# One scatter or gather at a time on GpSimd, each behind the landing of the one before

## The chip, the cores and the metric

The kernel runs on one core of a Trainium2 chip. The metric is the device time of one execution in microseconds (us), taken as the median of several runs without the profiler. The core has TensorE (PE, matrix products), VectorE (DVE), ScalarE (ACT), GpSimd (POOL) and SyncE (SP, here only an issuer of DMA transfers). The engines run their own instruction streams in order and meet at semaphores.

## The reference, cut to what matters

One transformer block with adaptive layer norm over x of 32 x 256 x 128 float32 (32 batches of 256 tokens):

```
mod = silu(c) @ wmod                       # six rows of 128 per batch: sa, ca, ga, sb, cb, gb
h = layernorm(x) * (1 + ca) + sa
x = x + ga * attention(h)                  # 16 heads of 8, rms-normed Q and K, gated heads
h = layernorm(x) * (1 + cb) + sb
x = x + gb * experts(h)                    # 32 experts, top 2 of a softmax router

def experts(x):                            # T = 8192 tokens
    rw = softmax(x @ router_w.T)
    vals, idx = top_k(rw, 2)
    w_masked = zeros_like(rw).at[arange(T)[:, None], idx].set(vals)
    for w_e, W_e in zip(w_masked.T, expert_weights):
        acc = acc + (x * w_e[:, None]) @ W_e
```

## The kernel before, in words

**Steps.** The work is a software pipeline over 32 batches. Step s handles batch s in stage 0 (b0), batch s-1 in stage 1 (b1) and so on to b8; there are 40 steps (`STEPS`), of which 0 to 34 are attention steps (`DRAIN` is 35) and 35 to 39 drain steps, and behind them come turns that finish the experts. Every engine has an `attention_step` that lists its tasks in the order in which it runs them. That order is written by hand, engine by engine.

**The experts.** The batches 0 to 29 are sparse: each token's row of h2 (128 floats) is sent to a slot in its expert's region in DRAM (`xs_d`), once per chosen expert. A batch has 2 x 128 tokens and two choices, hence four scatters k = 0 to 3 of 128 rows (64 KB) each, one index per partition from `slot`. Four chunks of batches (0-7, 8-15, 16-23, 24-29) have regions of their own. Behind a chunk a table of units of 128 rows is made, SyncE loads four units at a time (`xs_sb`, L650), TensorE transposes and multiplies them with the expert's weights (L2117, L2132), ScalarE stores them in `ys_d`. Then GpSimd gathers a batch's rows back, again four transfers k = 0 to 3 of 128 rows (`yg`, L921, indices `gidx`), and VectorE weighs and adds them (`combine`, L1620 to L1630). Expert groups run from step 16 on, two in each attention step. In attention steps, gathers of one batch stand in each of steps 25 to 34 (`combined_in(s)`), none earlier. The batches 30 and 31 are computed densely at the end.

**GpSimd's stream.** It does arithmetic on tiles and issues the indirect transfers: `scatter` (L906) and `gather` (L921). In an attention step before the change: gathers k=0 and 1 (of the batch combined in this step); scatter k=3 of b7; `x_plus_bias`(b4, L822), `scale_wo`(b4, L831), `copy_v`(b2, L752), `keep_slot`(b7, L896), `scale_wqkv`(b0, L763); `low_part`(b1, L794); gather k=2; `chosen`(b6, L864), `scale_ln2`(b5, L838), `keep_index`(b6, L881), `chosen_ranks`(b6, L873), `shift_ln2`(b5, L847); `max_lead`, `max_lead_wide`, `max_rest`(b2, L801, L808, L814); gather k=3; scatters k=0 and 1 of b6, `keep_weights`(b8, L888), scatter k=2 of b6, `less_largest`(b6, L855 and L856), and `norm_qk`(b0, L781) twice. A scatter waits for `slot_d` (VectorE's slot numbers, L1500) and adds 16 to `scat[batch's parity]` on landing, 64 per batch; a gather adds 16 to `yg_ld[n % 4]`, 64 per batch. In the steps without gathers only the four scatters remain.

**Who waits for GpSimd.** `norm_qk` gives `qn`, which TensorE transposes early in the next step (`transpose_qk`, L1924); ScalarE (`high_part`, L1070, `middle_part`, L1077), VectorE (`rest_part`, L1386) and GpSimd (`low_part`) split it in three bfloat16 parts, SyncE stores the parts (L602, L605) and loads them as `q_aug` and `k_aug` (L622, L626), and TensorE's `scores_q` (L1937) of the same batch needs them late in that step; VectorE's maxima of these scores (L1397) come ahead of the Newton steps that end in `rstd` (L1313), for which the next `norm_qk` waits. `max_rest` gives `msplit` to TensorE's `transpose_max` (L1946), then ScalarE and a transfer, for `scores_k`. `chosen` gives `mask` to `count_before`; `shift_ln2` gives `h2` to `transpose_h2` (L2020). ScalarE's `router_exp` (L1141) waits for `keep_weights`, and `less_largest` waits for that `router_exp`. TensorE's `probs_v` (L1986) gives four heads at a time to ScalarE's copy `out_transposed` (`oT`, L1095). VectorE copies the units' table (L1545) behind a small matmul of TensorE (L2104).

**SyncE and the queues.** SyncE issues the loads and stores in a written order; it waits for the scatters only ahead of a chunk's first group (`rows_complete`, L639), which stands eight or more steps behind them. `shift_ln2` and `slot_number` also wait for the scatters of the batch two earlier. GpSimd's transfers have a queue of their own, and share the core's 16 DMA engines with SyncE's and ScalarE's.

Of the kernel before, what the change touches and what calls it, by code (L numbers as in the profile page):

```python
# [60 lines left out]
FB = 4  # L61
# [25 lines left out]
def chunk_of(n):  # L87

    return next(k for k in CHUNKS if k.lo <= n < k.hi)
# [131 lines left out]
def build(nc, x, Wq, bq, Wk, bk, Wv, bv, Wo, bo, qn_w, kn_w, router_w, expert_w, c_in, wmod, out):  # L221
# [16 lines left out]
    with ctx:  # L238
# [203 lines left out]
        scat = [sem(f"scat{i}") for i in range(2)]  # L442
# [284 lines left out]
        def _(gp):  # L727
# [165 lines left out]
            def keep_slot(b):  # L893
                wait(gp, slot_d, b.n + 1)
                gp.nop(nofuse=True)
                nc.gpsimd.tensor_copy(slot_all[:, bass.ts(b.n, TOPK * TB)], slot[:, b.par]).then_inc(slota_d, 1)  # L896

            @of_sparse
            def scatter(b, k):

                chunk = chunk_of(b.n)
                if chunk.c >= SETS and b.n == chunk.lo and k == 0:
                    gp.wait_ge(xsT_ps, CHUNKS[chunk.c - SETS].base + CHUNKS[chunk.c - SETS].groups)
                wait(gp, slot_d, b.n + 1)
                gp.nop(nofuse=True)
                nc.gpsimd.indirect_dma_start(xs_d[chunk.set], bass.IndirectOffsetOnAxis(ap=slot[:, b.par, k:k + 1], axis=0),  # L906
                                             h2[:, b.par, k % TB, :], None).then_inc(scat[b.par], 16)

            def gather(n, ks):

                chunk = chunk_of(n)
                if n == chunk.lo and ks[0] == 0:
                    gp.wait_ge(look, 4 * (chunk.c + 1))
                    for i in range(YB):
                        gp.wait_ge(yt_st[i], 16 * groups_until(chunk.base + chunk.groups, i))
                if ks[0] == 0:
                    wait(gp, mix_d, MIX * (n - FB) + 2 * TB)
                gp.nop(nofuse=True)
                for k in ks:
                    pair = n * TOPK * TB + k  # L920
                    nc.gpsimd.indirect_dma_start(  # L921
                        yg[:, n % FB, k, :], None, ys_d[chunk.c],
                        bass.IndirectOffsetOnAxis(ap=gidx[:, pair:pair + 1], axis=0)).then_inc(yg_ld[n % FB], 16)

            def gather_in(s, *ks):

                for n in combined_in(s):
                    gather(n, ks)

            def attention_step(s, ahead, b0, b1, b2, b3, b4, b5, b6, b7, b8):  # L930

                gather_in(s, 0, 1)
                scatter(b7, 3)
                x_plus_bias(b4)
                scale_wo(b4)
                copy_v(b2)
                keep_slot(b7)
                past_first(scale_wqkv, b0)
                low_part(b1)
                gather_in(s, 2)  # L940
                chosen(b6)
                scale_ln2(b5)
                keep_index(b6)
                chosen_ranks(b6)
                shift_ln2(b5)
                max_lead(b2)
                max_lead_wide(b2)
                max_rest(b2)
                gather_in(s, 3)
                scatter(b6, 0)  # L950
                scatter(b6, 1)
                keep_weights(b8)
                scatter(b6, 2)
                less_largest(b6)
                norm_qk(b0, 0)
                norm_qk(b0, 1)

            def drain_step(s, ahead, b0, b1, b2, b3, b4, b5, b6, b7, b8):

                if s == DRAIN:  # L960
                    scatter(b7, 3)
                for k in range(TOPK * TB):
                    scatter(b6, k)
                gather_in(s, 0, 1, 2, 3)
# [1307 lines left out]
```

## Time and profile before

| | us |
|---|---|
| median of 3 runs without the profiler | 832.31 (829.86 to 837.1) |
| span of the profiled execution, first to last instruction | 977.1 |
| TensorE busy in it | 751.6 (77%) |
| VectorE busy | 676.2 (69%) |
| ScalarE busy | 564.5 (58%) |
| GpSimd busy | 507.0 (52%) |
| mean granted TensorE clock, share of full speed | 0.886 |

The profiled execution took longer than those without the profiler. Every duration below is from that one execution. In timeline rows the columns are start, duration, engine, line, operation, output and inputs with shapes, number of instructions merged, and in brackets the idle time of that engine just before and what ended it ("issue" is time in which it waited for nothing that the profile shows, "remote" an event of which the profile doesn't know the sender). Matmul ends are modelled. The duration of a DMA_INDIRECT is GpSimd's time for issuing it, not the movement of the data.

### The profile page before, as it was taken

The numbers are of one execution on the slowest core, as the hardware profiler recorded it, in microseconds if no ns is written. First come the engines' busy times: TensorE is split into PE (matmuls) and PEld (weight loads), VectorE is DVE, ScalarE is ACT, GpSimd is POOL, SyncE is SP. The second block draws the span as 40 slices with busy tenths as digits, with TensorE's granted clock in tenths as the row PEclk, the third lists the DMA queues.
The fourth block names the chain that finished last, engine by engine and source line by source line (L and its number), as shares of the span: only waits on it lengthen the run. The fifth ranks groups of instructions, "written<-read, shape, count | busy, mean of one in ns | idle before, by whom it ended". The sixth has DMA issues, their size and how long they took to land.

```text
span 977.1 us, 23375 instructions
## 1 busy us (share of the span) xinstructions
PE 751.6 (77%) x6334; PEld 512.0 (52%) x6334; DVE 676.2 (69%) x2015; ACT 564.5 (58%) x1300; POOL 507.0 (52%) x846
## 2 busy tenths in 40 slices
PE   4668988988888889998889788887988762524765
PEld 1234655545554566665666555564655551514665
DVE  4757878878786878788888687788876252611556
ACT  3156877776775778877778676676666522512100
POOL 5112455566654555555556666676665535273253
PEclk8579999999997999999999999999898765766888
DMA  2555545466444567767566666665554433754632
GB/s 66 146 146 142 117 115 148 120 150 151 123 115 122 152 168 183 179 175 181 158 179 177 178 161 172 162 167 152 152 154 122 128 108 86 211 154 133 183 81 81
DMA packets 178001, 141.70 MB, mean 145 GB/s; under 512 B 19540, under 2 KB 162612, under 8 KB 177876
## 3 DMA queue, kind: packets, MB, share of 16 engines
q1 hardware_dynamic: 122804, 99.54, 39.8%
q10 hardware_dynamic: 47392, 24.92, 8.8%
q0 software_dynamic: 7680, 15.74, 5.8%
q8 instruction: 57, 0.93, 0.5%
q14 instruction: 68, 0.56, 0.2%
HBM read 81.77 MB, written 57.80 MB: 143 GB/s over the span
## 4 chain that ended last, share of the span: by engine, by line
PE 39%; DVE 15%; issue 14%; DMA 9%; another core or an unknown queue 9%; SPq 7%; ACT 5%; POOL 1%; ACTq 0%; DVEq 0%; POOLq 0%
PE mx_ps L1937 10%; PE st_ps L1972 7%; PE o_ps L1986 6%; DVE negmax L1397 5%; DMA k_aug<-k_d 4%; DMA k_d<-parts 4%; PE st_ps L2132 3%; SPq L650 2%; PE misc L1995 2%; PE misc L1910 2%; SPq L602 2%; ACT pr L1089 2%; PE st_ps L2117 1%; PE misc L2029 1%
## 5 line engine op out<-in xcount | busy, mean ns | idle before, releaser
L1397 DVE TENSOR_REDUCE negmax<-mx_ps 128x2 f32<-128x512 f32 x512 | 339.0, 686 | 123.4 <-PE mx_ps L1937 68.1
L1089 ACT ACTIVATE pr<-st_ps 128x512 f32<-128x512 f32 x512 | 285.2, 599 | 77.9 <-PE st_ps L1972 71.9
L1937 PE MATMUL mx_ps<-k_aug,q_aug 126*128 126x256 bf16 x1024 | 200.1, 287 | 68.0 <-DVE negmax L1397 26.0
L1972 PE MATMUL st_ps<-q_aug,k_aug 128*128 128x256 bf16 x1024 | 190.5, 285 | 0.8 <-ACT ys_sb L1151 0.3
L1986 PE MATMUL o_ps<-pr,v_aug 128*32 128x256 f32 x2048 | 145.7, 404 | 37.4 <-issue 31.4
L921 POOL DMA_INDIRECT yg<-ys_d,gidx x120 | 117.7, 981 | 95.6 <-DVE yb L1627 42.0
L1937 PEld LDWEIGHTS mx_ps<-k_aug,q_aug 126*128 126x128 bf16 x1024 | 84.3, 100 | 158.3 <-issue 148.2
L906 POOL DMA_INDIRECT xs_d<-h,slot x120 | 120.5, 1004 | 59.2 <-DVE slot L1500 33.9
L1972 PEld LDWEIGHTS st_ps<-q_aug,k_aug 128*128 128x128 bf16 x1024 | 101.4, 105 | 30.1 <-issue 11.1
L1986 PEld LDWEIGHTS o_ps<-pr,v_aug 128*32 128x32 f32 x2048 | 57.3, 112 | 89.2 <-issue 69.5
L1095 ACT ACTIVATE oT<-o_ps 128x256 f32<-128x256 f32 x128 | 49.2, 384 | 77.7 <-remote 43.3
L781 POOL TENSOR_TENSOR qn<-qkvg,rstd 128x256 f32<-128x256 f32 x64 | 39.1, 635 | 83.3 <-DVE rstd L1313 83.3
L2117 PE MATMUL st_ps<-ident,xs_sb 128*128 128x128 f32 x248 | 41.9, 299 | 34.8 <-DMA xs_sb<-xs_d 22.0
L794 POOL TENSOR_TENSOR parts<-rest,parts 128x512 bf16<-128x512 f32 x32 | 37.1, 1158 | 52.5 <-ACT parts L1077 52.5
L1910 PE MATMUL misc<-wq_b,hT 128*128 128x400 f32 x128 | 58.5, 545 | 1.0 <-ACT hT L1028 0.9
L1151 ACT ACTIVATE ys_sb<-mx_ps 128x512 f32<-128x512 f32 x25 | 14.9, 596 | 65.7 <-remote 42.6
L2117 PEld LDWEIGHTS st_ps<-ident,xs_sb 128*128 128x128 f32 x248 | 32.2, 156 | 37.8 <-issue 37.1
L1995 PE MATMUL misc<-ident,oT 128*128 128x128 f32 x256 | 43.3, 297 | 10.9 <-ACT oT L1095 7.4
L1146 ACT ACTIVATE xsT<-st_ps 128x512 f32<-128x512 f32 x62 | 36.5, 596 | 24.2 <-PE st_ps L2117 20.1
L2132 PE MATMUL mx_ps<-we,xsT 128*128 x200 | 37.2, 347 | 13.8 <-ACT xsT L1146 9.9
L2132 PE MATMUL st_ps<-we,xsT 128*128 x296 | 42.6, 288 | 2.8 <-issue 1.4
L1366 DVE TENSOR_TENSOR qkvg<-misc,bias_p 128x400 f32<-128x400 f32 x64 | 36.0, 564 | 12.0 <-PE misc L1910 6.7
(192 smaller groups left out, 1280.3 us busy)
## 6 DMA issues: line engine op xcount, KB each, us to landing
xs_sb<-xs_d SPq DMA_DIRECT2D x248, 64.0 KB
ys_d<-ys_sb ACTq DMA_DIRECT2D x62, 256.0 KB
q_aug<-q_d SPq DMA_DIRECT2D x64, 192.0 KB
mod_o<-mod_d SPq DMA_DIRECT2D x32, 256.0 KB
bias_p<-bias_d SPq DMA_DIRECT2D x32, 200.0 KB
q_d<-parts SPq DMA_DIRECT2D x32, 192.0 KB, 2.1
k_d<-parts SPq DMA_DIRECT2D x32, 192.0 KB, 2.5
k_aug<-k_d SPq DMA_DIRECT2D x64, 96.0 KB
```

What stands on the lines that cost most here:

```text
L906: nc.gpsimd.indirect_dma_start(xs_d[chunk.set], bass.IndirectOffsetOnAxis(ap=slot[:, b.par, k:k + 1], axis=0), h2[:, b.par, k % TB, :], No ...
L921: nc.gpsimd.indirect_dma_start(yg[:, n % FB, k, :], None, ys_d[chunk.c], bass.IndirectOffsetOnAxis(ap=gidx[:, pair:pair + 1], axis=0)).the ...
L1089: nc.scalar.activation(pr[:, h % PR], st_ps[score_bank(b, h)][:], ACT.Exp, scale=SCALE).then_inc(exp_d, 1)
L1095: nc.scalar.activation(oT[:, g, :], o_ps[:, 0:NT], ACT.Copy).then_inc(oT_d, 1)
L1397: v.tensor_reduce(negmax[:, :, h], mx_ps[h % 2][:], AX.X, ALU.max, negate=True).then_inc(mx_d, 1)
L1910: t_.matmul(bank[:, 0:QKVG], hT[:, t * P:(t + 1) * P], wq_b[:, b.par], start=True, stop=True).then_inc(qkv_ps, 1)
L1937: last = t_.matmul(mx_ps[h % 2][:, qc], q_aug[b.par][0:MROW, h, qc * P:(qc + 1) * P], k_aug[b.par][0:MROW, h, :], start=True, stop=True)
L1972: last = t_.matmul(st_ps[score_bank(b, h)][:, kc], k_aug[b.par][:, h, kc * P:(kc + 1) * P], q_aug[b.par][:, h, :], start=True, stop=True)
L1986: last = t_.matmul(o_ps[32 * j:32 * j + VW, 0:NT], v_aug[b.par][:, kc, h, :], pr[:, h % PR, kc, :], start=(kc == 0), stop=(kc == TB - 1))
L1995: last = t_.transpose(bank[:, g * P:(g + 1) * P], oT[:, g, qc * P:(qc + 1) * P], ident[:])
L2117: last = t_.transpose(in_bank(g)[:, k * P:(k + 1) * P], xs_sb[:, g % XB, k, :], ident[:])
L2132: last = t_.matmul(out_bank(g)[:, k * P:(k + 1) * P], xsT[g % XB][:, k * P:(k + 1) * P], we[:, bass.ds(columns[k], P)], start=True, stop=True)
```

## The change

In the attention steps each scatter and each gather waits, before it is issued, until the scatter or gather issued last by GpSimd has landed (`behind_last`). They stand in other places of GpSimd's list: never two of them without a wait, and arithmetic between most. Scatter k=2 of a batch moves into the following step, beside k=3. The drain steps and the turns behind them issue as before, without that wait; the first drain step issues scatter k=2 as well.

```diff
+            asked = []
+
+            def behind_last():
+
+                if asked:
+                    gp.wait_ge(*asked[-1])
+
             @of_sparse
-            def scatter(b, k):
-
+            def scatter(b, k, alone=False):
+
+                if alone:
+                    behind_last()
...
+                asked.append((scat[b.par], 64 * b.nth + 16 * (k + 1)))
+
+            def gather(n, ks, alone=False):
+
+                if alone:
+                    behind_last()
...
+                    asked.append((yg_ld[n % FB], 64 * (n // FB) + 16 * (k + 1)))
+
+            def gather_in(s, *ks, alone=False):
 
                 for n in combined_in(s):
-                    gather(n, ks)
+                    gather(n, ks, alone)
 
             def attention_step(s, ahead, b0, b1, b2, b3, b4, b5, b6, b7, b8):
 
-                gather_in(s, 0, 1)
-                scatter(b7, 3)
+                scatter(b7, 2, True)
                 x_plus_bias(b4)
                 scale_wo(b4)
                 copy_v(b2)
                 keep_slot(b7)
                 past_first(scale_wqkv, b0)
+                gather_in(s, 0, alone=True)
                 low_part(b1)
-                gather_in(s, 2)
+                scatter(b7, 3, True)
                 chosen(b6)
                 scale_ln2(b5)
                 keep_index(b6)
+                gather_in(s, 1, alone=True)
                 chosen_ranks(b6)
                 shift_ln2(b5)
+                gather_in(s, 2, alone=True)
                 max_lead(b2)
                 max_lead_wide(b2)
                 max_rest(b2)
-                gather_in(s, 3)
-                scatter(b6, 0)
-                scatter(b6, 1)
+                gather_in(s, 3, alone=True)
+                scatter(b6, 0, True)
                 keep_weights(b8)
-                scatter(b6, 2)
                 less_largest(b6)
+                scatter(b6, 1, True)
                 norm_qk(b0, 0)
                 norm_qk(b0, 1)
 
             def drain_step(s, ahead, b0, b1, b2, b3, b4, b5, b6, b7, b8):
 
                 if s == DRAIN:
+                    scatter(b7, 2)
                     scatter(b7, 3)
```

## Rows read from the trace of the kernel before

**Rows 1.** The page: the chain that ended last, shares by engine.
```profile
PE 39%; DVE 15%; issue 14%; DMA 9%; another core or an unknown queue 9%; SPq 7%; ACT 5%; POOL 1%; ACTq 0%; DVEq 0%; POOLq 0%
```

**Rows 2.** Windows by stage: steps 7-13, 14-24, 25-34, the rest; length, busy per engine.
```profile
core 0: us, PE busy (x) PEld busy (x) DVE busy (x) ACT busy (x) POOL busy (x), PEclk, DMA share, GB/s
137.50:285.30 147.80, 129.71 (x1153) 80.48 (x1153) 118.84 (x363) 105.92 (x253) 86.46 (x160) 0.93 0.52 131
285.30:534.20 248.90, 220.81 (x2022) 150.47 (x2022) 201.50 (x601) 186.38 (x432) 136.42 (x254) 0.96 0.63 164
534.20:785.00 250.80, 203.86 (x1820) 138.08 (x1820) 176.73 (x546) 164.20 (x382) 157.39 (x258) 0.92 0.58 154
785.00:977.10 192.10, 101.71 (x652) 90.33 (x650) 83.96 (x267) 36.74 (x67) 81.64 (x84) 0.74 0.45 131
```

**Rows 3.** Groups of GpSimd by line and form: busy us, mean ns, idle before.
```profile
L906 POOL DMA_INDIRECT xs_d<-h,slot x120 | 120.5, 1004 | 59.2 <-DVE slot L1500 33.9 <-issue 23.1
L921 POOL DMA_INDIRECT yg<-ys_d,gidx x120 | 117.7, 981 | 95.6 <-DVE yb L1627 42.0 <-issue 28.4 <-DMA ys_d<-ys_sb 16.0
...
L855 POOL TENSOR_TENSOR dlg<-lg,top 128x64 f32<-128x64 f32 x29 | 8.5, 295 | 19.1 <-issue 18.7
```

**Rows 4.** Timeline, end of a step without gathers.
```profile
415.87 1.07 PE L1986 MATMUL o_ps<-pr,v_aug 128*32 128x256 f32 x16
415.92 1.02 POOL L906 DMA_INDIRECT xs_d<-h,slot  x1 [1.25 <-DVE slot L1500]
...
418.60 0.98 POOL L906 DMA_INDIRECT xs_d<-h,slot  x1 [0.16 <-issue]
418.78 0.38 ACT L1095 ACTIVATE oT<-o_ps 128x256 f32<-128x256 f32 x1 [1.24 <-remote]
...
419.55 1.44 DVE L1397 TENSOR_REDUCE negmax<-mx_ps 128x2 f32<-128x512 f32 x2 [1.78 <-remote]
```

**Rows 5.** Timeline, head of the step after it.
```profile
421.93 1.22 POOL L781 TENSOR_TENSOR qn<-qkvg,rstd 128x256 f32<-128x256 f32 x2 [1.37 <-DVE rstd L1313]
...
423.30 1.02 POOL L906 DMA_INDIRECT xs_d<-h,slot  x1 [0.15 <-issue]
...
424.04 0.67 DVE L1397 TENSOR_REDUCE negmax<-mx_ps 128x2 f32<-128x512 f32 x1
```

**Rows 6.** Timeline, a step with gathers and the head of the next.
```profile
667.73 1.16 POOL L794 TENSOR_TENSOR parts<-rest,parts 128x512 bf16<-128x512 f32 x1 [1.67 <-ACT parts L1077]
...
678.68 1.01 POOL L921 DMA_INDIRECT yg<-ys_d,gidx  x1 [0.40 <-DVE slot L1500]
...
683.26 0.38 ACT L1095 ACTIVATE oT<-o_ps 128x256 f32<-128x256 f32 x1 [2.62 <-remote]
...
688.33 1.01 POOL L921 DMA_INDIRECT yg<-ys_d,gidx  x1
...
691.95 0.74 POOL L822 TENSOR_TENSOR xga<-x_o,mod_o 128x256 f32<-128x256 f32 x1
```

**Rows 7.** Timeline, drain steps: the first of 16 gathers, and the table's copy.
```profile
800.55 0.98 POOL L921 DMA_INDIRECT yg<-ys_d,gidx  x1 [0.30 <-issue]
...
824.02 0.41 DVE L1545 CAST table<-misc 1x256 int32<-1x256 f32 x1 [21.64 <-remote]
```

**Rows 8.** A lone scatter and the window of its bytes; a gather and its user.
```profile
182.18 1.02 POOL L906 DMA_INDIRECT xs_d<-h,slot  x1
...
183.75:184.00 0.25, 0.25 (x2) 1.00 0.75 262
...
863.65 0.95 POOL L921 DMA_INDIRECT yg<-ys_d,gidx  x1 [0.30 <-issue]
...
866.30 0.48 DVE L1620 TENSOR_SCALAR yw<-yg,p_all 128x128 f32<-128x128 f32 x2 [0.30 <-issue]
```

**Rows 9.** Waits: GpSimd from 130 to 785 us, and one of TensorE's whole span.
```profile
POOL mask L864 <- DVE oh L1459: 49.0, 21, 6.3
...
POOL mlead L801 <- DVE negmax L1397: 25.9, 25, 1.8
...
PEld misc L1946 <- POOL msplit L814: 12.0, 22, 0.8
```

More of the change, by code:

```diff
@@ L907, in scatter @@
                                              h2[:, b.par, k % TB, :], None).then_inc(scat[b.par], 16)
-            def gather(n, ks):
+                asked.append((scat[b.par], 64 * b.nth + 16 * (k + 1)))
+            def gather(n, ks, alone=False):
+                if alone:
+                    behind_last()
                 chunk = chunk_of(n)
@@ L923, in gather @@
                         bass.IndirectOffsetOnAxis(ap=gidx[:, pair:pair + 1], axis=0)).then_inc(yg_ld[n % FB], 16)
-            def gather_in(s, *ks):
+                    asked.append((yg_ld[n % FB], 64 * (n // FB) + 16 * (k + 1)))
+            def gather_in(s, *ks, alone=False):
                 for n in combined_in(s):
-                    gather(n, ks)
+                    gather(n, ks, alone)
             def attention_step(s, ahead, b0, b1, b2, b3, b4, b5, b6, b7, b8):
-                gather_in(s, 0, 1)
-                scatter(b7, 3)
+                scatter(b7, 2, True)
                 x_plus_bias(b4)
```

## The prediction

> **What bounds the kernel now.** I read four views in this order: the chain that ended last, the windows by stage, the waits, and stretches of the timeline. The chain is led by TensorE (39%), but 14% is "issue" and 9% is "another core or an unknown queue" [rows 1]. The windows say how much of the attention steps TensorE does not fill: 147.8 - 129.7, 248.9 - 220.8 and 250.8 - 203.9 us, together 93 us of 647.5, at mean clocks of 0.93, 0.96 and 0.92 [rows 2]. After 785 us it fills only 101.7 of 192.1 us at 0.74.
>
> The timeline shows where these 93 us lie. GpSimd's indirect DMAs take about 1.0 us each (1004 ns for a scatter, 981 ns for a gather) [rows 3]. In a step without gathers three scatters are issued, the first at 415.92, the last at 418.60 us. The matmul group of probs_v ended by its record at 416.94, yet ScalarE's copy of it starts at 418.78 after a wait of 1.24, and VectorE stands 1.78 us until 419.55, both put down to "remote" [rows 4]. So results of TensorE come about 2.4 us later than their records say while scatters follow each other. Behind a lone scatter (423.30) VectorE's next maximum starts at 424.04 with no idle time [rows 5]. In a step with gathers there are two bunches: four transfers from 678.68, with ScalarE waiting 2.62 us until 683.26, and three from 688.33 [rows 6]. Where 16 gathers stand in a row, from 800.55, VectorE waits 21.64 us for a transposition [rows 7]. I count 19 steps without gathers (6 to 24) and 10 with (25 to 34): 19 x 2.4 = 46, 10 x (1.8 + 2.6) = 44, sum 90, which is the 93 us that TensorE doesn't fill.
>
> **The recorded execution is not the timed one.** Its span is 977.1 us, the median is 832.31: 144.8 us less, where what lies around a span would make the time longer. What could vanish without the recorder is the 90 us; the lost clock, (1-0.93) x 147.8 + (1-0.96) x 248.9 + (1-0.92) x 250.8 = 40; in the tail the 21.6 and, by an estimate from the tail's unfilled 90 us, some 35 more. That is 187 us, more than the 145 that must vanish. I therefore take it that the stall behind bunches is mostly the record's, and that the timed execution has at most (187 - 145)/187 = 0.22 of it, unless other losses exist that only the record has. This is the choice on which the forecast hangs.
>
> **The change part by part.** It removes no transfer and adds none: 8 per step with gathers, 4 without. One scatter per step crosses into the next step.
>
> *Steps without gathers.* Removed ahead of norm_qk: scatter k=2, 1.0 + 0.3 us. Added: scatter k=1 waits for the landing of k=0, with keep_weights and less_largest between, three instructions of at most 0.3 us each (295 ns for the longest [rows 3]), about 0.9 with gaps. When does one land? A scatter that starts at 182.18 moves its bytes around 183.75 to 184.0, that is 1.6 to 1.8 us after its start; a gather starting at 863.65 had landed when VectorE used it at 866.30, so by 2.65 [rows 8]. I take 2.2 us from start to semaphore, ends 1.8 and 2.65. The wait is then 2.2 - 1.0 - 0.9 = 0.3 us (0 to 0.8), against 1.3 us of issue moved away. norm_qk waits for VectorE's rstd by 1.37 us in such a step [rows 5], so both vanish. Scatter k=2 takes the place that k=3 had at the head; k=3 now stands behind low_part, ahead of chosen, which waits 49 us over 21 times for one_hot in these stages (2.3 us each) [rows 9]; 1.0 us fits. Sum 0; bounds -0.3 to +0.3 us per step by whether rstd or GpSimd comes last.
>
> *Steps with gathers.* At the head two transfers go: the issue of three took 691.95 - 688.33 = 3.6 us ahead of x_plus_bias [rows 6], now one takes 1.0 + 0.15, while gather k=0 comes back (1.15) behind scale_wqkv. low_part could start 3.6 - 2.3 = 1.3 us earlier. Recorded it waited 1.67 us for ScalarE [rows 6], but with the bunch of that stretch taking no TensorE time, GpSimd itself would be late: low_part heads the road through the parts and the loads to scores_q of the same batch. I count -1.3 us, bounds -1.3 and 0.
> Against this: gather k=3 and scatter k=0 are neighbours, so the landing is waited for openly: 2.2 - 1.0 = 1.2 for 0.3, +0.9 us; scatter k=1 +0.3. Behind it stand keep_weights (router_exp and ScalarE wait for it), less_largest, norm_qk and the whole next head. Between the other neighbours lies 1.0 to 2.5 us of arithmetic after the issue, start to start 2.3 us or more, so at 2.2 they don't wait. Gather k=2 now stands ahead of max_lead, which waits 25.9 us over 25 times, 1.0 each [rows 9]: 1.15 us fits within 0.15 (gather k=1 ahead of chosen_ranks has no one waiting so directly). TensorE waits for max_rest (12.0 us over 22 times [rows 9]), so this 0.15 counts twice over. Sum: -1.3 + 0.9 + 0.3 + 0.3 = +0.2 us per step; with a landing of 1.8: -0.7; with 2.65: each of seven neighbours pays up to 0.4 more, +2.9.
> Total of the forecast case: 10 x 0.2 = 2 us, minus a few us of a remnant of the stall: 0, so 832 us, with 10 x (-0.7) and 10 x 1.2 (2.4 us landing) around it: 822 to 844.
>
> The first drain step gets one scatter more, 1.3 us, on a GpSimd that stands idle for over 10 us there. The rows of 16 and 24 gathers behind the attention steps are not touched.
>
> The Trainium skill (SBUF — State Buffer, "Who interferes with whom") says that only VectorE and GpSimd share a port and that TensorE never waits on anyone. Rows 4 and 7 show TensorE's results late beside GpSimd's transfers, so for the recorded execution the trace contradicts it; by that rule nothing is to be gained from spreading the transfers, which is the forecast case.
>
> **The rivals.**
> A. *The stall behind bunches is real in part.* For it: the record ties it to bunches in every such step, and lone transfers have none. Against it: 187 us must lose 145. Removable are 90 + 40 = 130 us of attention steps. At the share of 0.22 that is 29 us, less 2: 805 us. If the recorder also slows the loads (so that less of the 145 falls to the stall), a share of 0.4 gives 52 us, 782 us. This decides from a share of 0.08 on (10 us).
> B. *The landing waits make GpSimd's own round the longest.* In a step with gathers it is busy 157.4/10 = 15.7 us [rows 2]; with five gaps of 0.3 between neighbouring transfers and an estimate of 0.15 us for each of 13 other hand-overs that is 19.2 us. TensorE's work is 220.8/11 = 20.1 us per step [rows 2]. With landings 2.65 us after the start, eight waits add some 2.9 us: 22.1 us, over TensorE's round by 2.0; with the loads' traffic on the same 16 DMA engines landings may take 3 us, for 24. What waits is TensorE at transpose_max. Price 10 x 2 = 20 us, 852 us; it decides from a landing of about 2.3 us on. Against it: a quiet landing is faster, and the head gets 1.3 us back.
> C. *It does something else than it says:* the awaited value could be reached early, as two batches share a semaphore by parity. The values count 64 per batch and 16 per transfer, in issue order, so each wait is for the last one issued. I leave this at no chance of its own.
>
> **How the numbers follow.** Forecast case 0.41, its own range 822 to 844. A 0.34, centre 805, from 782 to 823. B 0.25, centre 850, from 841 to 870. A measurement of this kernel tells 1% (8 us) from no change. Faster by over 1%: 0.31 of A and 0.04 of the forecast case, 0.35. Slower: 0.22 of B and 0.04 of the forecast case, 0.26. Within: 0.39. The range for 8 in 10 leaves out the lower fifth of A and the upper part of B: 790 to 856.
>
> **What would show it.** In the profile after, "remote" waits of oT and negmax at the ends of steps shrink to under 0.5 us, the clock of the attention steps rises toward 1, and the recorded span falls by 60 to 110 us, far more than the time: this gap shows that the stall is the record's. If time and span fall alike, A holds. Under B, mlead and msplit have no idle time ahead of them in steps 25 to 34, TensorE's wait for msplit there grows beyond 1 us a step, and the idle time ahead of scatter k=0 is over 1.5 us. low_part's wait for ScalarE should grow at the head of gather steps if the 1.3 us is real. The prediction is wrong if the time leaves 822 to 844.

## The result, and the profile after

The changed kernel takes 1000.37 us (992.23 to 1006.21) beside 834.7 us for the kernel before: a ratio of 1.197, 95% interval 1.189 to 1.206. The forecast was 832, within 790 to 856. It was wrong by 168 us, on the side of rival B and far past its price.

One thing is needed to read the numbers below. The kernel before has two speeds, by the chip it runs on. Its recorded trace [rows 1 to 9] has a span of 977.1 us; on two chips of the experiments it took 975 to 979.5 us, on a third 836, and in the measurement of the change 834.7. I call the first kind the 977 chips and the other the 835 chip. The trace of the changed kernel comes from the 835 kind (it has no "remote" wait, and its time came back on that chip), so it must not be held against [rows 2] directly. An experiment below records the kernel before on the 835 chip; its rows take the place of [rows 2] in the comparison.

The groups of GpSimd's transfers in the changed kernel, as in [rows 3] (busy us, mean ns, idle before them and what ended it):

```profile
L915 POOL DMA_INDIRECT xs_d<-h,slot x120 | 121.2, 1010 | 217.5 <-DMA xs_d<-h,slot 112.6
...
L933 POOL DMA_INDIRECT yg<-ys_d,gidx x120 | 119.3, 994 | 93.0 <-DMA yg<-ys_d,gidx 38.1
```

The transfers themselves cost what they did: 1010 and 994 ns against 1004 and 981. The idle time ahead of the scatters rose from 59.2 to 217.5 us. The waits of GpSimd say for what. First the 19 steps without gathers (116.48 to 543.47 us), then seven of the ten with gathers (to 780.21 us); columns: us in total, times, longest:

```profile
POOL xs_d L915 <- DMA xs_d<-h,slot: 76.8, 24, 5.2
POOL dlg L855 <- issue: 31.4, 18, 1.9
...
POOL h L847 <- DMA xs_d<-h,slot: 12.4, 15, 2.7
```

```profile
POOL xs_d L915 <- DMA yg<-ys_d,gidx: 40.7, 14, 5.1
POOL yg L933 <- DMA yg<-ys_d,gidx: 26.0, 14, 3.4
POOL xs_d L915 <- DMA xs_d<-h,slot: 25.2, 13, 4.3
POOL yg L933 <- DMA xs_d<-h,slot: 10.0, 6, 1.9
```

In the seven steps the four landing waits sum to 101.9 us, 14.6 a step. The last row of the first list is a wait that the kernel before had too (`shift_ln2`, for the scatters of the batch two earlier). It sums to 12.4 us here, to 9.9 with one landing wait a step (below) and to 0.5 in the new order without any, so it comes with the waits; scatter k=3 stands shortly ahead of shift_ln2.

GpSimd's timeline shows one such step, its transfers alone:

```profile
644.62 1.02 POOL L915 DMA_INDIRECT xs_d<-h,slot  x1 [4.21 <-DMA xs_d<-h,slot]
645.67 1.22 POOL L781 TENSOR_TENSOR qn<-qkvg,rstd 128x256 f32<-128x256 f32 x2
647.70 1.00 POOL L915 DMA_INDIRECT xs_d<-h,slot  x1 [0.81 <-DMA xs_d<-h,slot]
...
651.31 1.02 POOL L933 DMA_INDIRECT yg<-ys_d,gidx  x1 [0.16 <-issue]
...
655.16 0.99 POOL L915 DMA_INDIRECT xs_d<-h,slot  x1 [1.46 <-DMA yg<-ys_d,gidx]
...
659.67 1.64 POOL L933 DMA_INDIRECT yg<-ys_d,gidx  x1 [1.95 <-DMA xs_d<-h,slot]
...
663.99 1.09 POOL L933 DMA_INDIRECT yg<-ys_d,gidx  x1 [1.52 <-DMA yg<-ys_d,gidx]
...
667.43 0.97 POOL L933 DMA_INDIRECT yg<-ys_d,gidx  x1 [1.31 <-DMA yg<-ys_d,gidx]
...
672.76 1.00 POOL L915 DMA_INDIRECT xs_d<-h,slot  x1 [4.36 <-DMA yg<-ys_d,gidx]
...
677.79 1.02 POOL L915 DMA_INDIRECT xs_d<-h,slot  x1 [2.75 <-DMA xs_d<-h,slot]
```

Read it by the starts: 647.70 - 644.62 = 3.08 us, then 3.61, 3.85, 4.51, 4.32, 3.44, 5.33 and 5.03. Eight such stretches make the round, 33.2 us (from norm_qk at 645.67 to norm_qk at 678.84). What counts is what ended them: seven of the eight transfers start when the one ahead has landed. The eighth, the gather at 651.31, has arithmetic of its own length ahead of it. So the arithmetic between the transfers lies inside the landings, but for that one place.

How long is a landing? For the scatters of this kernel the profile gives the time from the start of the issue to the landing: shortest, median, longest.

```profile
DMA to landing us min/median/max: 2.2/3.0/6.7
```

The scatter at 644.62 landed after 2.3 us and the next one started after 3.08; the scatter at 426.04 below landed after 5.8 and the next one started after 6.55. The difference is 0.8 us, and it is the same (0.77 to 0.83 us) all 52 times that a transfer stood behind the landing of a scatter in this trace. A wait for a landing therefore costs, from start to start, the landing and 0.8 us more.

At a head without gathers one wait is long, the one that the prediction did not cost:

```profile
426.04 1.00 POOL L915 DMA_INDIRECT xs_d<-h,slot  x1 [1.01 <-DMA xs_d<-h,slot]
427.07 1.22 POOL L781 TENSOR_TENSOR qn<-qkvg,rstd 128x256 f32<-128x256 f32 x2
432.59 1.01 POOL L915 DMA_INDIRECT xs_d<-h,slot  x1 [4.30 <-DMA xs_d<-h,slot]
```

From scatter k=1 to scatter k=2 are 6.55 us (4.7 to 7.5 over the heads of these steps), with 1.2 us of arithmetic in them. x_plus_bias, scale_wo, copy_v, scale_wqkv and low_part stand behind it. The head of a step with gathers has the same instructions and takes 3.08 us at 644.62, so it isn't the arithmetic between that makes the landing long. The windows of the two heads, the step with gathers first (the column before the last is the busy share of the DMA engines):

```profile
644.62:647.70 3.08, 0.75 (x4) 0.75 (x5) 0.00 (x0) 0.00 (x0) 2.24 (x3) 0.57 0.34 112
426.04:432.59 6.55, 6.35 (x62) 4.84 (x61) 5.96 (x18) 5.85 (x13) 2.22 (x3) 1.00 0.89 202
```

### The profile page after: what moved, and what is told of

Its sections match the earlier page's. It is cut to its first block and busy times, and to the rows that moved or that the text cites. A ratio compares the mean times of both kernels' runs of the same rounds, so it can differ in the third digit from the quotient of the medians.

```text
span 1004.4 us, 23410 instructions
## 1 busy us (share of the span) xinstructions
PE 759.4 (76%) x6334; PEld 514.6 (51%) x6334; DVE 699.4 (70%) x2015; ACT 567.2 (56%) x1300; POOL 511.5 (51%) x846
## 5 line engine op out<-in xcount | busy, mean ns | idle before, releaser
L1952 PE MATMUL mx_ps<-k_aug,q_aug 126*128 126x256 bf16 x1024 | 197.4, 288 | 60.3 <-DVE negmax L1412 29.0
L915 POOL DMA_INDIRECT xs_d<-h,slot x120 | 121.2, 1010 | 217.5 <-DMA xs_d<-h,slot 112.6
L1952 PEld LDWEIGHTS mx_ps<-k_aug,q_aug 126*128 126x128 bf16 x1024 | 86.9, 101 | 143.0 <-issue 132.3
L2001 PE MATMUL o_ps<-pr,v_aug 128*32 128x256 f32 x2048 | 148.2, 410 | 2.7 <-ACT oT L1110 2.1
L2147 PE MATMUL st_ps<-we,xsT 128*128 x296 | 53.7, 339 | 3.8 <-issue 3.4
L1939 PE MATMUL misc<-ident,qn 128*128 128x128 f32 x128 | 24.5, 323 | 37.7 <-POOL qn L781 37.0
L2147 PEld LDWEIGHTS st_ps<-we,xsT 128*128 128x128 f32 x296 | 47.8, 244 | 10.2 <-issue 9.9
L2010 PEld LDWEIGHTS misc<-ident,oT 128*128 128x128 f32 x256 | 30.9, 147 | 31.3 <-ACT oT L1110 28.8
L2147 PE MATMUL mx_ps<-we,xsT 128*128 x200 | 35.0, 334 | 13.6 <-ACT xsT L1161 12.4
```

What stands on the lines that cost most here:

```text
L1952: last = t_.matmul(mx_ps[h % 2][:, qc], q_aug[b.par][0:MROW, h, qc * P:(qc + 1) * P], k_aug[b.par][0:MROW, h, :], start=True, stop=True)
L2001: last = t_.matmul(o_ps[32 * j:32 * j + VW, 0:NT], v_aug[b.par][:, kc, h, :], pr[:, h % PR, kc, :], start=(kc == 0), stop=(kc == TB - 1))
L2010: last = t_.transpose(bank[:, g * P:(g + 1) * P], oT[:, g, qc * P:(qc + 1) * P], ident[:])
L2147: last = t_.matmul(out_bank(g)[:, k * P:(k + 1) * P], xsT[g % XB][:, k * P:(k + 1) * P], we[:, bass.ds(columns[k], P)], start=True, stop=True)
```

## The experiments

**The landing waits step by step, and the order without them.** Run on a 977 chip in one measurement, where the kernel before took 978.6 us. The first keeps the new order and takes every wait away:

```diff
             def behind_last():
-                if asked:
-                    gp.wait_ge(*asked[-1])
+                return
```

> The new order on GpSimd without any of the waits. Theory W (the waits for the landings cost the time; in the trace after, a transfer issued behind a wait starts 3.1 to 7.4 us after the one before, where I had taken 2.2): about 834 us, between 820 and 845, the time of the kernel before. Rival O (the new places cost it: scatter k=2 at the head, gather k=0 ahead of low_part, gather k=1 and 2 ahead of chosen_ranks and max_lead): 900 us or more. On the recorded execution: if transfers in a bunch hold up TensorE only while recorded, this kernel, which has neighbours only at gather k=3 / scatter k=0, should show a span within 3% of its time, where the kernel before has 977 us recorded against 834 timed.

Measured: 908.7 us, ratio 0.930 [0.923, 0.936]. On this chip the order alone saves 7%. By its number this is the rival's time (900 or more), yet it is a gain: both expectations start from a kernel before at 834 us, and here it takes 978.6. So do the times expected for the next three, of which only the differences can be compared.

The next two keep the waits in the ten steps with gathers only, and in the others only:

```diff
+                waiting[0] = bool(combined_in(s))      # the other kernel: not combined_in(s)
...
-                if asked:
+                if asked and waiting[0]:
```

> The kernel after, with the waits only in the ten steps that have gathers (25 to 34). Theory W: steps 25 to 34 of the trace after take 33 to 36 us, against an estimate of 21 in the timed kernel before; so most of the loss is here: 834 + 10 x 13 = about 960 us, 940 to 975. A rival by which every step loses alike (166 us over 29 steps, 5.7 us each) gives 834 + 57 = 891 us.

> The kernel after, with the waits only in the steps that have no gathers (6 to 24). Theory W: what remains of 166 us, 834 + 35 = about 870 us, 855 to 890; the head's scatter k=2 there waits 3 to 5 us in each step. Every step alike: 834 + 19 x 5.7 = 942 us. The losses of this kernel and of the one with waits in gather steps alone should add up to the 166 us if they don't interact.

Measured: 1014.9 us with the waits in the steps with gathers (+106 over order-only, expected +126), 948.3 us with them in the others (+40, expected +35). The fourth puts the waits into the order of the kernel before:

```diff
-                gather_in(s, 0, 1)
-                scatter(b7, 3)
+                gather_in(s, 0, alone=True)
+                gather_in(s, 1, alone=True)
+                scatter(b7, 3, True)
```

(and so on for the other transfers of the step)

> The order of the kernel before, with a wait for the landing ahead of each transfer of the attention steps. Theory W: here five pairs per gather step are neighbours and pay their whole landing (at least 3.1 us from start to start, and over 4 beside the loads) instead of two: slower than the kernel after, 1040 us or more. Rival O (the new places cost the time, the waits little): 834 to 870 us.

Measured: 1182.7 us, ratio 1.209 [1.201, 1.217]. Its waits of a scatter for the landing of a scatter sum to 214.1 us alone. With the waits in both, the new order is 123 us faster than the old one (1059.2 below): it softens the waits, it does not pay for them.

**The changed kernel on the same chip.** The unchanged text of the changed kernel, with order-only beside it again (before: 974.9 us).

> The changed kernel itself, beside the kernel before. In the measurement of the change the kernel before took 834.7 us and this one 1000.4; in the first four experiments the kernel before took 978.6, as in its recorded execution (977.1), so the kernel before has two speeds from chip to chip. If the kernel before is at 978 here: the other experiments predict 1015 + 948 - 909 = 1054 us for this one (waits in either kind of step, added up), so a ratio of about 1.08. If the kernel before is at 834 here: 1000 us again.

> The new order without the waits once more (908.7 us beside 978.6 of the kernel before in the first set). If the kernel before is at 978 here: 909 again. If it is at 834: theory S (the stall of TensorE behind bunches exists only where the kernel before is slow, and spreading the transfers saves that stall and nothing else) expects the ratio to vanish: 834 us within 2%. The rival, that the order by itself saves 7% anywhere, expects 775.

Measured: 1059.2 us, ratio 1.087 [1.078, 1.095], and 908.2 us. The waits cost 151 us; the two halves above give 106 + 40 = 146, so they nearly add up. The last max_rest of the attention steps starts at 829.28 us here and at 828.66 us in the first trace of the changed kernel. Up to there it takes the same time on either kind of chip; the 56 us between 1060.3 and 1004.4 lie in the tail, which has no landing waits. The waits of the two kernels for "remote" on this chip, the changed one first:

```profile
ACT ys_sb L1166 <- remote: 47.2, 6, 16.4
...
DVE table L1560 <- remote: 21.6, 1, 21.6
```

```profile
ACT ys_sb L1165 <- remote: 49.0, 5, 15.1
DVE table L1559 <- remote: 21.6, 1, 21.6
...
ACT oT L1109 <- remote: 6.5, 4, 2.4
```

oT had 43.3 us of these and negmax 42.5 in the recorded trace of before, over 21 and 18 waits. Order-only has 6.5 for oT and none for negmax: spreading the transfers between arithmetic removes nearly all of these late results of TensorE, with no wait for a landing. The rows of the tail, which is as it was, stay.

**Waits in the tail alone.** The order-only kernel, with a landing wait ahead of each gather of the drain steps and of what follows:

```diff
             def behind_last():
-                return
+                if asked and drained[0]:
+                    gp.wait_ge(*asked[-1])
...
-                gather(n, range(TOPK * TB))
+                for k in range(TOPK * TB):
+                    gather(n, [k], True)
```

> The new order without waits in the attention steps, and with a wait ahead of each gather of the drain steps and behind them, where 16 to 24 stand in a row. Theory S, where the kernel before is at 978: the tail's stalls (one of 21.6 us in the recorded execution, some 50 in all) shrink, GpSimd has idle time there: 909 - 30 = about 880 us. Where the kernel before is at 834: no stall to save, landings of 3.1 us for issues of 1.26, 850 us or more. Rival: gathers in the tail are on the path either way, 930 us or more.

Measured: 1014.7 us instead of 908, a plain miss: the rival written beside it (930 or more) is what came. The stall did go (ys_sb has 0.4 us left, the table's row is absent), but the gathers now stand one landing apart:

```profile
752.99 0.94 POOL L935 DMA_INDIRECT yg<-ys_d,gidx  x1 [2.38 <-DMA yg<-ys_d,gidx]
756.23 0.94 POOL L935 DMA_INDIRECT yg<-ys_d,gidx  x1 [2.30 <-DMA yg<-ys_d,gidx]
759.50 0.94 POOL L935 DMA_INDIRECT yg<-ys_d,gidx  x1 [2.33 <-DMA yg<-ys_d,gidx]
```

This is the cleanest price of a wait in the study: 3.24 and 3.27 us from start to start, nothing else on GpSimd between them and the DMA engines 0.11 and 0.08 busy. Without the wait a gather costs 1.26 us there.

**One wait a step, at the head.** Order-only, with the wait ahead of scatter k=2 alone, on the 977 chip and later on the 835 chip:

```diff
-                return
+                if asked and head[0]:
+                    gp.wait_ge(*asked[-1])
```

> The new order with a single wait per step, ahead of scatter k=2 at the head, which in the trace after waits 3 to 5 us in each of the steps without gathers and 0.8 to 1.3 in those with. Theory W: this one wait explains nearly all of the loss in steps without gathers (948.3 - 908.7 = 40 us there), so about 909 + 40 = 950 us where the kernel before is at 978. Rival: GpSimd's slack absorbs a wait behind norm_qk, since nothing there is due soon: 909 to 920.

> One landing wait in a step, ahead of scatter k=2 at its head. On the stalling chip it cost 60 us over 30 steps (967.7 against 908), 2 us a step, though the head's wait is 4 us long. If that is GpSimd's round overtaking TensorE's, it is the same wherever it runs: 890 to 910 where order-only takes 840. If part of it was a clash with the stall, it costs under 30 us here.

Measured: 967.7 us on the 977 chip (+60) and 908.9 us on the 835 chip, where order-only takes 845.1 (+64). The one wait that the prediction took for free costs about 2 us a step, and its price does not depend on the stall. In the windows used below, the 19 steps without gathers take 419.56 us with this wait alone, 382.25 with none and 423.74 with all of them: it makes 37 of the 41 us that the waits cost there.

**The kernel before, order-only and the changed kernel on the 835 chip.**

> The kernel before, unchanged, profiled again. The recorded trace of it has a span of 977 us with 'remote' waits of oT, negmax and ys_sb (136 us together) and of the table copy (21.6 us), while its timed runs of the measurement of the change took 834. Theory 'two speeds by chip': where it takes 830 to 840, its span agrees within 2 us and none of the remote waits is there; where it takes 970 to 980 they all are, at the same size as in the recorded trace. Rival 'the profile itself brings the stall': span 970 or more and remote waits beside times of 835.

> The new order without landing waits. On the chip of the first two measurements it took 908 where the kernel before took 975 to 979. On a chip where the kernel before takes 835, theory 'the order pays only by breaking up the bunches that stall': 830 to 850, ratio 0.99 to 1.02, as the kernel with lighter loads (843) suggests. Rival 'the order is worth 7% anywhere': 775 to 790.

> The changed kernel again, beside order-only: their difference is what the landing waits cost. On the chip of the second measurement 1059 - 908 = 151 us. Where the kernel before takes 835: 1000 for the changed kernel, so 150 to 165 us for the waits alone, and 46 us above the same kernel with light loads (954). If order-only were itself slow there (870 or more) the waits would cost under 130.

Measured: 835.8, 845.1 and 998.8 us; order-only against before 1.0125 [1.009, 1.016], the changed kernel 1.195 [1.190, 1.200]. So the loss is split: the new order costs 9 us, the landing waits 154 us.

The windows of the three show where. Both windows of a kernel run from a start of norm_qk to a start of norm_qk: the 19 steps without gathers, then seven with. Columns as in [rows 2]; first the kernel before:

```profile
115.47:490.12 374.65, 347.76 (x3335) 231.27 (x3335) 336.05 (x1013) 307.72 (x719) 233.30 (x433) 1.00 0.66 168
490.12:644.65 154.53, 140.32 (x1322) 96.76 (x1321) 137.56 (x413) 121.38 (x281) 115.67 (x191) 0.99 0.74 192
```

Order-only:

```profile
115.35:497.60 382.25, 352.42 (x3341) 233.94 (x3341) 340.31 (x1014) 308.72 (x720) 235.40 (x432) 0.99 0.65 165
497.60:654.42 156.82, 140.97 (x1323) 97.53 (x1322) 139.16 (x413) 121.97 (x281) 118.11 (x189) 0.99 0.74 188
```

The changed kernel:

```profile
118.27:542.01 423.74, 362.52 (x3342) 238.64 (x3342) 358.31 (x1014) 309.36 (x720) 234.36 (x433) 0.98 0.60 149
542.01:777.24 235.23, 167.79 (x1329) 110.21 (x1327) 141.22 (x423) 122.57 (x283) 117.11 (x189) 0.83 0.50 127
```

A step with gathers takes 154.53/7 = 22.1, 22.4 and 33.6 us; one without 19.7, 20.1 and 22.3. GpSimd is busy 116 to 118 us in the seven in all three, so it does no more work; it waits. TensorE's share falls from 91% to 71% and its granted clock from 0.99 to 0.83. Its busy time grows by 27 us, from 140.97 to 167.79, for the same instructions, at the lower granted clock. TensorE still stands idle for 67 of the 235 us; whether the longer matmuls cost time of their own was not separated.

Against [rows 4 and 7]: the trace of before on this chip has no "remote" wait at all. The same two places there, the end of a step without gathers and the table's copy:

```profile
406.10 0.98 POOL L906 DMA_INDIRECT xs_d<-h,slot  x1 [0.16 <-issue]
...
406.65 0.38 ACT L1095 ACTIVATE oT<-o_ps 128x256 f32<-128x256 f32 x1 [0.26 <-PE o_ps L1986]
...
407.26 1.28 DVE L1397 TENSOR_REDUCE negmax<-mx_ps 128x2 f32<-128x512 f32 x2
```

```profile
715.04 1.38 POOL L921 DMA_INDIRECT yg<-ys_d,gidx  x1 [0.30 <-issue]
716.19 0.41 DVE L1545 CAST table<-misc 1x256 int32<-1x256 f32 x1 [0.60 <-PE misc L2104]
```

Three scatters back to back and 16 gathers in a row, as in [rows 4 and 7], yet the copies of TensorE's results start 0.26 and 0.60 us after their records allow, not 1.24 and 21.64. The span is 833.6 and this profiled run took 835.3 us, so the profile does not slow the kernel either.

**Why the landings are long: lighter loads.** Two loads of each step that fill 128 partitions from one row of DRAM (256 and 200 KB) are cut to 16 partitions, from batch 2 on. It leaves out 7/8 of those rows, so these batches are computed from old ones.

```diff
-                sp.dma_start(bias_p[:, b.par], row.partition_broadcast(P)).then_inc(bp_ld[b.par], 16)
+                rows = P if b.n < 2 else 16
+                sp.dma_start(bias_p[0:rows, b.par], row.partition_broadcast(rows)).then_inc(bp_ld[b.par], 16)
...
+                    sp.dma_start(mod_o[0:16, b.par].rearrange("p a f -> p (a f)"),
+                                 mod_d[b.n, GA * P:(GA + 4) * P].partition_broadcast(16)).then_inc(xo_ld[b.par], 16)
```

> The changed kernel, with two loads of each step cut: the rows of mod_o and of bias_p, which are spread over 128 partitions (256 and 200 KB in a step), reach only 16 partitions from batch 2 on. It leaves out 7/8 of those loads. Theory A (a landing that takes 3.1 us in a quiet stretch takes 4 to 7 us at the end of a step because its packets share the DMA engines with the loads of the step): the wait ahead of scatter k=2 at the head falls from some 4 us to 1 or 2, and of the 1059 us of the changed kernel on this chip 40 to 60 go, while the order-only kernel with the same cut goes from 908 to 895 at the lowest. Theory B (the landing is long by itself, or by the GpSimd instructions between, whatever else moves): 1050 to 1060, and the head's wait stays at 4 us.

> The new order without any landing wait, with the same two loads cut to 16 partitions. It is the other half of the pair: what the lighter loads are worth where nothing waits for a landing. Theory A: 895 to 908. Theory B: the same. If it falls as far as the changed kernel does with this cut, the gain there isn't from the landings.

It ran on the 835 chip (before: 836.5 us), so the base is 998.8 and 845.1, not the 1059 and 908 of the expectation. Measured: 954.0 us for the changed kernel, 45 less; 842.9 us for order-only, 2 less. So the gain is in the landings: 43 of the 154 us that the waits cost. GpSimd's waits over the 19 steps without gathers, with lighter loads:

```profile
POOL xs_d L920 <- DMA xs_d<-h,slot: 43.0, 26, 2.6
```

and a head of a step in it:

```profile
422.28 1.00 POOL L920 DMA_INDIRECT xs_d<-h,slot  x1 [0.28 <-issue]
423.31 1.22 POOL L786 TENSOR_TENSOR qn<-qkvg,rstd 128x256 f32<-128x256 f32 x2
426.95 1.01 POOL L920 DMA_INDIRECT xs_d<-h,slot  x1 [2.42 <-DMA xs_d<-h,slot]
```

The longest wait fell from 5.6 to 2.6 us, their sum from 79 to 43; start to start it is 4.7 us here. The same head in the changed kernel, on the same chip, 7.1 us from start to start:

```profile
426.51 1.00 POOL L915 DMA_INDIRECT xs_d<-h,slot  x1 [0.28 <-issue]
427.54 1.22 POOL L781 TENSOR_TENSOR qn<-qkvg,rstd 128x256 f32<-128x256 f32 x2
433.62 1.01 POOL L915 DMA_INDIRECT xs_d<-h,slot  x1 [4.86 <-DMA xs_d<-h,slot]
```

From start to start the heads of 18 steps without gathers took 5.0 to 7.8 us before the cut and 3.7 to 4.9 after it. In the stretch from 426.51 to 433.62 the DMA engines were 0.87 busy, from 422.28 to 426.95 with the lighter loads 0.66. So a wait costs 3.1 to 3.3 us where the DMA engines are quiet (0.08 to 0.34 busy in the stretches shown), and up to 7.8 us where the loads of the step keep them busy. The loads are not shown to be all of it. In the quiet head at 644.62 VectorE stands idle as well; in the two heads compared here it is equally busy (6.07 of 7.11 us and 3.90 of 4.67), so the 2.4 us between them go with the loads, but what makes the landing 3.9 us with the lighter loads and 2.3 in the quiet head was not separated.

Of the 45 us, 27.8 come from the 19 steps without gathers (1.5 a step) and 11.9 from the seven with (1.7 a step); at 223.3/7 = 31.9 us instead of 33.6, eight landings in series still exceed TensorE's round.

**Waits ahead of scatters k=0 and k=1 only.** The rest as in order-only.

```diff
-                if alone:
+                if alone and k < 2:
                     behind_last()
...
-                if alone:
-                    behind_last()
```

> The new order in the attention steps, with the landing waits ahead of the scatters k=0 and k=1 only; the gathers and the scatters k=2 and k=3 wait for nothing. Theory 'each wait costs its own length': the wait of k=0 behind the last gather (4.4 us in the sample) and that of k=1 (1.3 to 2.8 us) stay in the 10 gather steps, 1.0 us of k=1 in the 19 others: 908 + 60 + 15 = 980 to 990. Theory 'GpSimd's round has slack that the first waits fill': 910 to 940, since a round of GpSimd with two waits is still shorter than TensorE's.

On the 835 chip, so against 845.1, where the two expectations become +72 to +82 and +2 to +32. Measured: 901.3 us, +56, between them. The same windows give 387.7 us for the 19 steps (+5) and 201.1 us for the seven (+44, 6.3 us a step; the two waits themselves sum to 47.3 us there, 6.8 a step). In a step without gathers GpSimd had slack for nearly all of the wait of k=1 (12.7 us in the 19); in a step with gathers it had none.

**Arithmetic between the tail's gathers.** Order-only, with an addition of 256 columns on GpSimd ahead of each gather of the tail.

```diff
                 for k in ks:
+                    if len(ks) == TOPK * TB:
...
+                        nc.gpsimd.tensor_tensor(zeros[:, 0:256], zeros[:, 256:512], zeros[:, 512:768],
+                                                ALU.add).then_inc(spaced, 1)
```

> The order-only kernel, and in the drain steps and the turns of the tail an addition of 256 columns on GpSimd (some 0.7 us) ahead of each gather, so that no two of them stand back to back; nothing waits for a landing. If the stall of TensorE's results (ys_sb 49 us and table 21.6 us in the order-only kernel) comes from indirect transfers being issued back to back, both shrink and the time falls from 908 to 860 to 895. If it comes from how many are under way and not yet landed, a gap of 0.7 us is too short: ys_sb and table stay, and the time is 905 to 925.

It came to the 835 chip, where there is no stall to remove, so it answers nothing on the question. What it shows is the price of filling: 891.6 us against 845.1, 46 us for 80 additions of 0.74 us each. So the time that GpSimd takes for the gathers is on the road that ends the tail.

**The new order in the steps with gathers only.**

```diff
+                if list(combined_in(s)):
+                    step_apart(s, ahead, *b)
+                else:
+                    step_before(s, ahead, *b)
```

> The order of the kernel before in the steps without gathers, the new order in the 10 steps with gathers, no landing waits. Where the kernel before takes 836 and order-only 845: the round of GpSimd is 8 us longer over the 19 steps without gathers in order-only (382 against 374 from the starts of norm_qk) and not longer in the others, so 835 to 839 if the +9 lies in those 19 steps; 842 to 847 if it lies in the steps with gathers. Where the kernel before takes 975 and order-only 908: between them, 920 to 945, as the bunches of three scatters at the end of a step without gathers are back and the bunches of gathers are not. A version that beats both kernels on either chip would need under 832 and under 908.

It came to the other 977 chip (before: 979.5 us). Measured: 941.6 us, ratio 0.964 [0.958, 0.969]: of the 7% that the order saves there, about half is in the ten steps with gathers. Its trace says where the rest is: negmax waits 26.9 us for "remote" again, all of it in the 19 steps that have their old order back, and oT 15.1 us there against 5.1 in the seven with the new order. Whether the 9 us that the order costs on the 835 chip lie in the steps without gathers it could not say.

## Why the prediction was wrong

**"I take 2.2 us from start to semaphore, ends 1.8 and 2.65. The wait is then 2.2 - 1.0 - 0.9 = 0.3 us"** The price of a wait failed, in two ways. First, 2.2 us is the shortest landing, not the usual one: the scatters of the changed kernel landed after 2.2 us at the least, 3.0 in the median and 6.7 at the most, and over 2.65 in more than half of the cases. The sum took a quiet landing for one beside the loads of a step. Second, it put nothing for the way from the landing to the start of the next transfer, and that is 0.8 us each time. From start to start a wait therefore costs at least 3.1 us where it was taken for 2.2, 3.1 to 5.3 in the step with gathers shown, and 4.7 to 7.5 at the head of a step without. The Trainium skill (DMA: Bandwidth & Descriptors, "Anatomy of one DMA") gives about 2.0 us plus bytes over 436e3 per us for a transfer issued by GpSimd, which would be 2.15 for 64 KB; the quiet landings here, 2.2 to 2.3 us, agree, and the 0.8 us behind them is not part of it. Its statement in "Latency and other measured facts", that the fixed part is smaller when the load on HBM is lighter, agrees in direction with the lighter loads (7.1 to 4.7 us from start to start at one head), though no run here tells the load on HBM from the sharing of the DMA engines.

**"Scatter k=2 takes the place that k=3 had at the head."** A step left out of the sum: its wait follows scatter k=1 with only norm_qk's 1.2 us between. At 2.2 us it would have been free; at 4.7 to 7.5 it costs 2 us a step, 60 to 64 in all.

**"Between the other neighbours lies 1.0 to 2.5 us of arithmetic ... so at 2.2 they don't wait."** They do wait: in the seven steps 47 of the 56 transfers stood until the one ahead had landed. The sum should have been made the other way round: eight transfers in series were hidden at 8 x 2.2 = 17.6 us, under TensorE's 20.1, but they take 8 x 4.15 = 33 us, which is the step. Even quiet they would take 8 x 3.1 = 25 us, an estimate from the shortest stretches, and be the longer road. Arithmetic between them counts for nothing once that is so. By that estimate the chain crosses its limit at 20.1/8 = 2.5 us from start to start, shorter than any wait of the changed kernel.

**Rival B** was the mechanism; its price of 20 us was about an eighth of the 154, as it priced the landing at 2.65 to 3 us and the 0.8 at nothing. It also lay in the 19 steps without gathers (+41 us by the windows), where I had put zero. Its signs came as named: msplit waits for nothing but its neighbour, TensorE's wait for msplit is 26.8 us over seven steps, and the idle time ahead of scatter k=0 is 4.4 us in the step shown.

**"The recorded execution is not the timed one."** The numbers were right (977 against 832) and the inference was wrong. In every experiment the profiled run's span is within 2 us of its own time; what differs is the chip, and the recorded trace of before has the marks of a 977 chip (the same 21.6 us at the table's copy, where nine traces from the 835 kind have no "remote" wait at all). The stall is neither the recorder's nor present in the timed runs. That the timed runs are free of the stall came true by luck, since they ran on the fast kind of chip and not because they went without the recorder. The size of the stall was read loosely too: [rows 4] have oT 1.84 us behind the record of its matmul, and the 2.4 us of the sum aren't in them. The same windows on both kinds of chip give 417.70 against 374.65 us for the 19 steps and 178.68 against 154.53 for the seven: the slower kind loses 2.3 us in a step without gathers and 3.4 (not 4.4) in one with.

**Rival A** (the stall is real in part, 805 us) holds on a 977 chip and for order-only alone: 908 against 975, 7%. With the waits even that chip ends at 1.087. On the 835 chip there is nothing to gain, and the order costs 9 us. By the windows 7.6 of them lie in the 19 steps without gathers. A candidate is less_largest: its idle time with no shown cause is 44.9 us in order-only, 31.1 of it in those 19 steps, and 0.8 in the kernel before on the same chip, where scatter k=2 stood ahead of it. That was not tried alone.

**"-1.3 us (low_part earlier)".** Not confirmed: seven steps with gathers take 156.8 us in order-only and 154.5 in the kernel before on the 835 chip, so the head gives nothing back.

No version beats both kernels on both kinds of chip. Order-only is the best where the kernel before takes 977 (0.93), the kernel before is the best where it takes 835 (order-only 1.0125). Against order-only the landing waits lose on both, wherever in the step they stand: 40 us at the least.

## What to carry to other kernels

A wait for the landing of a transfer ahead of the next one turns an engine's queue of transfers into a chain: multiply the number of transfers in a round by what one wait costs, and hold that against the round of the busiest engine before anything else. One wait costs, from start to start, a landing under the load of that place and the time from there to the start of the next transfer (0.8 us here); a landing read in a quiet stretch is too short on both counts. If transfers in a bunch disturb another engine, put arithmetic between them and let them be in flight together; here that alone removed nearly all of the disturbance in the attention steps.

## What the runs showed of the hardware

The same kernel takes 836 us on one chip and 975 to 979.5 us on two others. On the slower ones TensorE's results reach ScalarE and VectorE late while indirect transfers are issued back to back: 21.6 us at the table's copy, the same figure in the recorded trace, in order-only, in the changed kernel and on the second slow chip. The profile calls the sender of these waits unknown, so that it is TensorE's result that comes late is read from what the waiting instruction needs. On the faster one the same sequence costs 0.60 us there. Why chips differ is open; the runs only show that it goes with bunches of indirect transfers, that arithmetic between them removes most of it (oT 43.3 to 6.5 us), and that a landing wait ahead of the tail's gathers removes it there too (ys_sb 49.0 to 0.4 us) at a far higher price, 107 us.

A scatter of 64 KB lands 2.2 us after the start of its issue in a quiet stretch and up to 6.7 us (7.0 in the second trace) beside the step's loads; the next transfer, if it waits for that, starts 0.8 us after the landing.
